# Counting products in four column tiles, and the second half's turn of an LSTM step cut in three pieces

## The reference, cut to what matters

```python
# L1_ffn: one sequence of T = 625 steps, batch 1, hidden size 512
combined = concat([x_t, h_prev])
f_t = sigmoid(combined @ W_f + b_f); i_t = sigmoid(combined @ W_i + b_i)
c_t = f_t * c_prev + i_t * tanh(combined @ W_c + b_c)
o_t = sigmoid(combined @ W_o + b_o)
h_t = o_t * tanh(c_t)
...
# L2_gnn: attention over edges with a bias per edge, a row maximum and sums by segment
logits = einsum(q[rows] * scale, k[cols]) + att_bias      # 10000 edges, 8 heads
row_max = segment_max(logits, rows); denom = segment_sum(p, rows)
```

## Time and profile before

| | us |
|---|---|
| median of 3 runs (4644.18 to 4644.81) | 4644.66 |
| the profiled execution | 4646.08 |
| its span in the profile | 4644.3 |
| TensorE matmuls busy (96% of the span) | 4446.2 |
| VectorE busy (50%) | 2307.4 |
| ScalarE busy (41%) | 1912.3 |
| GpSimd busy (8%) | 361.0 |
| mean granted TensorE clock | 0.971 of full speed |

### The profile page before, as it was taken

How to read it: one execution, slowest core, us unless ns; L and a number is a source line. 1 busy time by engine, 2 the same in 40 slices (tenths; PEclk the granted TensorE clock), 3 DMA queues, 4 the chain that set the end, 5 groups by cost and what they waited for, 6 DMA issues and landing times.

```text
span 4644.3 us, 136942 instructions
## 1 busy us (share of the span) xinstructions
PE 4446.2 (96%) x53052; PEld 2196.5 (47%) x53052; DVE 2307.4 (50%) x10628; ACT 1912.3 (41%) x7133; POOL 361.0 (8%) x351
## 2 busy tenths in 40 slices
PE   9888898999999999999999999999999998799999
PEld 7444554444444444444444444344446745555554
DVE  6424313666666666666666666566632524511111
ACT  0010111566666555666666555455531502111111
POOL 0000001000000222000000232013210001000000
PEclk9998899999999999999999999999999999799999
DMA  2000101620000000000000000000003302011111
GB/s 72 25 34 23 49 28 73 189 85 0 9 0 0 1 2 3 3 0 0 0 0 0 2 2 5 0 1 2 1 26 89 77 32 71 30 46 64 55 64 38
DMA packets 49646, 139.42 MB, mean 30 GB/s; under 512 B 25496, under 2 KB 33455, under 8 KB 38171
## 3 DMA queue, kind: packets, MB, share of 16 engines
q1 hardware_dynamic: 39325, 113.73, 7.5%
q0 software_dynamic: 10208, 24.08, 2.6%
HBM read 114.92 MB, written 22.60 MB: 30 GB/s over the span
## 4 chain that ended last, share of the span: by engine, by line
PE 93%; DVE 5%; ACT 1%; issue 1%; POOL 0%; DVEq 0%; ACTq 0%; POOLq 0%
PE PS L1007 48%; PE PS L724 32%; PE PS L1001 4%; PE PS L1063 3%; PE PS L810 2%; PE PS L1141 1%; PE PS L755 1%; PE PS L1191 1%; PE PS L1131 1%; PE PS L1121 1%; ACT BUF L1286 1%; DVE stats L1588 0%; PE PS L783 0%; DVE BUF L1684 0%; POOL BUF L599 0%
## 5 line engine op out<-in xcount | busy, mean ns | idle before, releaser
L1007 PE MATMUL PS<-BUF,ls_hid 128*1 128x256 f32 x40000 | 2310.0, 380 | 4.8 <-DVE ls_hid L2013 4.7
L1007 PEld LDWEIGHTS PS<-BUF,ls_hid 128*1 128x1 f32 x40000 | 927.3, 84 | 1182.4 <-DVE ls_hid L2013 209.8
L1983 DVE STREAM_TRANSPOSE ls_turn<-PS 128x192 f32<-128x192 f32 x1250 | 478.4, 383 | 547.1 <-PE PS L1007 547.0
L1405 ACT ACTIVATE ls_th<-ls_pr 128x1 f32<-128x1 f32 x2500 | 600.8, 287 | 100.9
L724 PE MATMUL PS<-ring,BUF 128*125 128x512 f32 (+1 forms) x1440 | 619.4, 589 | 23.2 <-DVE BUF L1729 5.8
L724 PE MATMUL PS<-BUF,ring 128*128 128x512 f32 (+1 forms) x2176 | 597.2, 436 | 2.3 <-ACT BUF L1286 1.4
L724 PEld LDWEIGHTS PS<-BUF,ring 128*128 128x128 f32 x2176 | 331.7, 192 | 274.3 <-issue 272.3
L2013 DVE SCALAR_TENSOR_TENSOR ls_hid<-ls_gate,ls_th 128x1 f32<-128x1 f32 x2500 | 345.1, 149 | 233.6 <-ACT ls_th L1405 214.4
L724 PEld LDWEIGHTS PS<-ring,BUF 128*125 128x125 f32 x1440 | 270.6, 190 | 353.2 <-issue 333.4
L1398 ACT ACTIVATE ls_gate<-ls_turn 128x6 f32<-128x6 f32 x1250 | 265.5, 212 | 320.4 <-DVE ls_turn L1983 240.7
L1294 ACT ACTIVATE BUF<-PS,cols 128x625 f32<-128x625 f32 x130 | 101.4, 782 | 625.6 <-PE PS L724 622.7
(11 more groups left out here) (312 smaller groups left out, 3092.8 us busy)
## 6 DMA issues: line engine op xcount, KB each, us to landing
cell_bias<-BUF SPq DMA_DIRECT2D x5, 2441.4 KB
BUF<-cell_bias POOLq DMA_DIRECT2D x5, 2441.4 KB, 15.0
ring<-in_L_wo SPq DMA_DIRECT2D x11, 1024.0 KB, 4.9
ring<-in_L_wi SPq DMA_DIRECT2D x8, 1024.0 KB, 4.9
ring<-in_L_wg SPq DMA_DIRECT2D x8, 1024.0 KB, 4.8
ring<-in_L_wout SPq DMA_DIRECT2D x8, 1024.0 KB, 4.8
gate_inputs<-BUF SPq DMA_DIRECT2D x5, 1344.0 KB
BUF<-in_L_wh SPq DMA_DIRECT2D x4, 1024.0 KB, 12.8
```

The costliest lines, as they stand in the source:

```text
L1007: ins = nc.tensor.matmul(ls_sum[u][f][32 * q:32 * q + 1, :].rearrange("p (j n) -> p j n", j=4), ls_hid[:, c:c + 1], ls_half[:, q, c, :, f, :],
L1405: nc.scalar.activation(ls_th[:, f, c:c + 1], ls_pr[:, f, c:c + 1], ACT.Tanh, scale=0.5, bias=ls_pr[:, f, 2 + c:3 + c]).then_inc(ls_tanh[f], 1)
L1983: V.transpose(ls_turn[:, f, 2:8, :], ls_sum[u][f][:, 64:256].rearrange("p (g n) -> p g n", g=6)).then_inc(ls_turned[f], 1)
```

## The change

`rank_add` issues each of its two products as four, one per strip of 32 output partitions (the last 29 wide), each a column tile of the array with its own 32 columns of `tri` or `rest`; all four take the same moving tile. It is eight products in place of two.

Half 1's turn of 192 columns is cut into `turn_if` (the 128 columns of gates i and f) and `turn_c` (the 64 columns of gate c). With `turn_o(1)` the half's sums are now turned in three pieces. `turn_if` stands in VectorE's queue between cell(0) and hidden(0,0), `turn_c` where turn(1) stood, between hidden(0,0) and hidden(0,1). Both wait for `ls_full[1]`. ScalarE's tanh of half 1's gates i, f, c waits for both pieces, by a new semaphore.

```diff
+        ls_turned_if = sem("ls_turned_if")
...
                     for a, b in ((0, 512), (512, N)):
-                        ins = nc.tensor.matmul(PS[0:EP, 1, a:b], m, hot_rank[u][:, a:b], start=False, stop=False,
-                                               skip_group_check=True)
+                        for p in range(0, EP, 32):
+                            e = min(p + 32, EP)
+                            ins = nc.tensor.matmul(PS[p:e, 1, a:b], m[:, p:e], hot_rank[u][:, a:b], start=False, stop=False,
+                                                   skip_group_check=True)
                     return ins
...
                 def gates(f, t):
+                    if f == 1:
+                        act.wait_ge(ls_turned_if, t + 1)
                     act.wait_ge(ls_turned[f], t + 1)
...
-                def turn(f, t, u):
-                    dve.wait_ge(ls_full[f], t + 1)
-                    V.transpose(ls_turn[:, f, 2:8, :], ls_sum[u][f][:, 64:256].rearrange("p (g n) -> p g n", g=6)
-                                ).then_inc(ls_turned[f], 1)
+                def turn(t, u):
+                    dve.wait_ge(ls_full[0], t + 1)
+                    V.transpose(ls_turn[:, 0, 2:8, :], ls_sum[u][0][:, 64:256].rearrange("p (g n) -> p g n", g=6)
+                                ).then_inc(ls_turned[0], 1)
+
+                def turn_if(t, u):
+                    dve.wait_ge(ls_full[1], t + 1)
+                    V.transpose(ls_turn[:, 1, 2:6, :], ls_sum[u][1][:, 64:192].rearrange("p (g n) -> p g n", g=4)
+                                ).then_inc(ls_turned_if, 1)
+
+                def turn_c(t, u):
+                    dve.wait_ge(ls_full[1], t + 1)
+                    V.transpose(ls_turn[:, 1, 6:8, :], ls_sum[u][1][:, 192:256].rearrange("p (g n) -> p g n", g=2)
+                                ).then_inc(ls_turned[1], 1)
...
                 def step(t, u, between=None):
-                    turn(0, t, u)
+                    turn(t, u)
                     turn_o(0, t, u)
                     product(0, t)
                     cell(0, t)
+                    turn_if(t, u)
                     hidden(0, 0, t)
-                    turn(1, t, u)
+                    turn_c(t, u)
                     hidden(0, 1, t)
                     turn_o(1, t, u)
                     halve(0, t)
```

## The result

| | median us | runs |
|---|---|---|
| before | 4644.46 | 4 (4644.18 to 4644.81) |
| changed | 4689.80 | 4 (4688.74 to 4690.97) |

The ratio is 1.0098, with a 95% interval of 1.0080 to 1.0115: 45 us slower. The forecast was 4714 in a range of 4678 to 4752. The profiled execution took 4689.48 us, with a span of 4687.7.

The account below looks back on a forecast made before the run. TensorE's work was taken to bound counting steps, the VectorE and ScalarE loop the others. New step: 1.30 + 0.235 + 0.22 + 2.41 = 4.165 us; -6, +58 and +18 make +70 us, so 4714 us, range 4678 to 4752.

Parts of the forecast that it names:

- `ls_full[1]` at +1.30: Half 1's sums come three add groups of 0.43 us after `ls_full[0]`, 1.30 us into the step, counted from turn(0).
- The hold of turn_if: On VectorE, turn_if keeps hidden(0,0) from starting for 0.235 us, halfway between 0.16 (64 columns) and 0.31 (192).
- hidden(0,0) to add(0,0): From the start of hidden(0,0) on VectorE to TensorE's first add: 0.22 us, read from a scatter step.
- add(0,0) to the next turn(0), 2.41: TensorE's stretch from the first add to the next step's first turn, without a stall: 2.41 us.
- turn_c and half 1: turn_c ends at +1.815 against +1.68 for turn(1), so half 1 is 0.135 us late, at no cost.
- the second stall: TensorE's 0.12 us wait inside the adds for hidden(1,0), in steps without counting; claimed gone, with 0.10 to spare.
- The count in tiles: TensorE's eight counting products take 0.35 us to the seeds, against 0.41 now, and fit in the 0.395 available.
- All kinds of step alike: Counting, scatter and plain steps all become 4.165 us, from 4.185, 3.925 and 3.88.
- Half 1 is not ready early: Denies the rival that `ls_full[1]` is there by +0.95 and turn_if fits VectorE's idle gap: 4564 us, chance 0.06.
- the tiles run side by side: Denies the rival that column tiles run one after another, the count taking 1.17 us: 4962 us, chance 0.04.
- the halves don't cancel: Denies the rival that both halves of the change sum to zero, needing a hold of 0.12 us: 4645 us, chance 0.02.
- no first turn waits behind ScalarE: Denies the rival of a new wait, rank_far or ScalarE's extra one, making counting steps 4.25 to 4.4 us: 4790, chance 0.04.

Follow-up runs that it names:

- the first experiment: The kernel before with only the counting products issued in four column tiles, turns left as they were: 4570.4 us, ratio 0.9829.

## Why the prediction was right, point by point

- **`ls_full[1]` at +1.30.** Right. turn_if starts at +1.29 to +1.30 in every kernel that has it and all eight products, whatever stood ahead of it, and where it stands ahead of hidden(0,0) with TensorE as its releaser; with one product less it starts at +0.94. One argument for it was thinner than it looked. The prediction held turn(1)'s 0.11 behind hidden(0,0) against the 0.04 behind hidden(0,1). But hidden(0,0) waits for its tanh, and behind such a one the queue is held for 0.08 (1701.23 to 1701.31, 1703.54 to 1703.62), so TensorE held turn(1) for only the last 0.03.
- **The hold of turn_if.** Right: 0.24 to 0.25 (1506.39 to 1506.64) against the 0.235 taken between two rows. The 192-column turn holds 0.31, also as read. The Trainium skill's rule, that the next op waits for the empty pipe (VectorE: DVE Perf Modes, "The DRAIN you can't avoid"), does not hold here: turn_if lasts 0.32, and hidden(0,0) starts after 0.24. The same section adds that a next op that is not held starts earlier, which the prediction left out and the trace agrees with.
- **hidden(0,0) to add(0,0), the term that was mis-sized.** Taken as 0.22 from the earlier trace rows, where hidden(0,0) waits for its tanh as its last semaphore. Behind turn_if the tanh is long there: hidden(0,0) takes 0.12 to 0.13 instead of 0.16 and the add follows after 0.18. 625 x 0.04 = 25 us, which is the whole distance between the forecast of +70 and the measured +45.
- **add(0,0) to the next turn(0), 2.41.** Right, 2.40 to 2.41.
- **turn_c and half 1.** Right in effect: the second stall is gone, the adds run through in 3.63. But the second wait on ScalarE, or the shorter piece, is not nothing: the tanh starts 0.09 behind the end of turn_c (1506.68 + 0.24 against 1507.01), where it was 0.04 behind turn(1). In the changed kernel this is covered; with turn_if behind hidden(0,0) it is part of the 45 us.
- **The count in tiles.** It fits under the wait, as said. Its price was too high: 0.27 where I took 0.35 and held 0.29 for the floor, and it starts 0.10 earlier, a gap ahead of it that I had not counted. In a counting step alone that is worth 0.24 us, as the first experiment says, not 0.10 to 0.15. The Trainium skill's rule that a change of tiling mode drains the array (TensorEngine Tiling (Array Packing), "Key Properties") agrees with both gaps going. That this is their cause is not shown: in tiles the weight loads also start 0.21 ahead of the product (1505.93 against 1506.14), where the whole ones started with it (1504.36), and no run separates the two. The wrong price cost nothing in the forecast, since the gain is covered.
- **All kinds of step alike.** Right: 4.12 and 4.13.
- **The rivals.** Half 1 is not ready early; the tiles run side by side; the halves don't cancel; and no first turn waits behind ScalarE: rank_far ended at +4.09 (1504.25 + 0.82, from a first turn at 1500.98), 0.06 later than forecast, and still nothing was late.

## What to carry to other kernels

Before an instruction is moved ahead of another in an in-order queue, ask when its semaphore comes, not whether the queue is idle there: count the producer's work behind the last known event (here three add groups of 0.43 us). An instruction that starts right behind another is not thereby held by it; look for the same pair elsewhere and see how short the distance can be, in a place where the first of them waits for the same thing (here 0.08 behind a hidden that waited, 0.04 behind one that did not). And test the parts of a change alone: here one part gains 1.7% and the other turns that into a loss of 1%, since a gain on an engine shows only while that engine is the bound.

## What the runs showed of the hardware that was not expected

- hidden(0,0), a VectorE instruction on a 128x1 column, takes 0.16 us where its last semaphore comes while it waits, and TensorE's first product follows 0.21 to 0.22 after its start; behind a transposition and with its semaphores already there it takes 0.12 to 0.13 and the product follows after 0.17 to 0.19. The next VectorE instruction starts 0.08 behind the first kind and 0.04 to 0.05 behind the second.
- The time for which a transposition of PSUM columns holds the next instruction: 0.31 us for 192 columns, 0.24 for 128, and for 64 columns 0.13 right behind another transposition and 0.16 behind a hidden, where it also lasts longer (0.24 against 0.21).
- Eight bf16 products of 512 and 113 columns in four column tiles take 0.27 us to the next product, and the two whole ones 0.41, with a further 0.10 ahead of them between the column-tiled adds and the whole product. The whole ones' weight loads start with the product, those in tiles 0.21 ahead of it.
